# A gated mixture and a GRU on one core: first `up` products ahead of the routing, four banks, the sum's halves apart, step 0 without products

## The reference

```python
gate_logits = concat([full_agg, hp_agg, wp_agg]) @ gate_w + gate_b
gate_logits = gate_logits * (1.0 + scale) + shift      # from silu(cond) @ time_w + time_b
w_be = top-2 of softmax(gate_logits), normalised       # one weight per sequence and expert
for e in range(E):
    h = gelu(x @ ew1[e] + eb1[e])                      # 256 -> 1024
    out += w_be[:, e] * mask[e] * (h @ ew2[e] + eb2[e])
x = x + out + gelu(x @ sw1 + sb1) @ sw2 + sb2
def step(h, ...):                                      # 1024 steps, h0 = 0
    z = sigmoid(xz + h @ U_z + vz); r = sigmoid(xr + h @ U_r + vr)
    hh = tanh(xh + (r * h) @ U + vh)
    return (1 - z) * h + z * hh
x = x + scan(step, x)
```

## Time and profile before

| | us |
|---|---|
| median of 3 runs | 1881.32 |
| lowest, highest | 1879.59, 1881.68 |
| the profiled execution | 1878.24 |
| its span, first to last instruction | 1876.4 |

### The profile page before, as it was taken

How to read it: one execution, slowest core, us unless ns; L and a number is a source line. 1 busy time by engine, 2 the same in 40 slices (tenths; PEclk the granted TensorE clock), 3 DMA queues, 4 the chain that set the end, 5 groups by cost and what they waited for, 6 DMA issues and landing times.

```text
span 1876.4 us, 101766 instructions
## 1 busy us (share of the span) xinstructions
PE 1844.4 (98%) x39969; PEld 1703.9 (91%) x39970; DVE 1454.8 (78%) x11505; ACT 713.4 (38%) x3785; POOL 199.4 (11%) x515
## 2 busy tenths in 40 slices
PE   8999999999999999999999999999999999999998
PEld 8998999989899998999989999899999989999766
DVE  5787878778787787877878787787877878788776
ACT  4333433434333343433434344343433434334322
POOL 0110101101020110101101011110101101011000
PEclk9999999999999999999999999999999999999999
DMA  9000000000000000000000000000000000000000
GB/s 321 4 4 5 5 4 5 5 4 5 5 5 5 4 5 5 4 5 5 4 5 5 4 5 5 4 5 5 4 5 5 4 5 5 5 5 4 5 5 4
DMA packets 16926, 23.62 MB, mean 13 GB/s; under 512 B 3585, under 2 KB 15160, under 8 KB 16445
## 3 DMA queue, kind: packets, MB, share of 16 engines
q1 hardware_dynamic: 15280, 17.05, 2.6%
q10 hardware_dynamic: 1164, 0.07, 0.0%
HBM read 15.01 MB, written 2.10 MB: 9 GB/s over the span
## 4 chain that ended last, share of the span: by engine, by line
PE 94%; DVE 2%; ACT 2%; issue 1%; ACTq 0%; DVEq 0%
PE up_ps L740 20%; PE y_ps L758 20%; PE r_ps L863 13%; PE c_ps L863 13%; PE r_ps L842 6%; PE z_ps L863 6%; PE c_ps L842 5%; PE z_ps L872 4%; ACT rc_tanh_ps L408 2%; PE y_ps L690 2%; DVE h_cur L662 1%; PE c_ps L774 1%; PE z_ps L774 1%; DVE p_cur L633 1%; PE r_ps L774 1%
## 5 line engine op out<-in xcount | busy, mean ns | idle before, releaser
L740 PE MATMUL up_ps<-feat,up_w 128*128 128x128 f32 x2528 | 519.2, 302 | 0.2
L758 PE MATMUL y_ps<-hidden,down_w 128*128 128x128 f32 x2528 | 515.4, 301 | 0.0
L839 PEld LDWEIGHTS <-u_high 128*128 128x128 f16 x4096 | 398.2, 97 | 20.7
L408 ACT ACTIVATE rc_tanh_ps<-r_ps 128x4 f32<-128x4 f32 x1024 | 161.8, 158 | 574.5 <-PE r_ps L863 574.4
L740 PEld LDWEIGHTS up_ps<-feat,up_w 128*128 128x128 f32 x2528 | 362.3, 190 | 1.2 <-ACT hidden L397 0.9
L758 PEld LDWEIGHTS y_ps<-hidden,down_w 128*128 128x128 f32 x2528 | 360.4, 190 | 0.0
L863 PEld LDWEIGHTS r_ps<-h_cur,u_mid 128*128 128x128 f16 x4096 | 252.1, 96 | 113.6 <-issue 46.6
L863 PE MATMUL c_ps<-p_cur,u_mid 128*128 128x40 bf16 (+10 forms) x4096 | 337.4, 179 | 0.0
L863 PE MATMUL r_ps<-h_cur,u_mid 128*128 128x20 bf16 (+5 forms) x4096 | 336.4, 178 | 0.0
L662 DVE TENSOR_TENSOR_SCAN h_cur<-rc_tanh_ps,blend 128x8 f32<-128x8 f32 x1024 | 178.0, 174 | 165.5 <-ACT rc_tanh_ps L408 165.4
L288 POOL TENSOR_TENSOR hidden<-hidden,expert_w 128x128 f32<-128x128 f32 (+3 forms) x416 | 163.9, 394 | 1339.0 <-ACT hidden L397 1339.0
(11 more groups left out here) (154 smaller groups left out, 4059.0 us busy)
## 6 DMA issues: line engine op xcount, KB each, us to landing
up_w<-in_L_cond_ew SPq DMA_DIRECT2D x4, 1024.0 KB, 9.3
down_w<-in_L_cond_ew SPq DMA_DIRECT2D x4, 1024.0 KB, 10.4
x_rows<-in_x SPq DMA_DIRECT2D x8, 256.0 KB, 4.6
out<-out_rows SPq DMA_DIRECT2D x128, 16.0 KB, 1.8
up_w<-in_L_cond_sw SPq DMA_DIRECT2D x1, 1024.0 KB, 12.7
down_w<-in_L_cond_sw SPq DMA_DIRECT2D x1, 1024.0 KB, 13.4
cf<-in_L_cond_C_r SPq DMA_DIRECT2D x1, 256.0 KB, 9.6
cf<-in_L_cond_C_z SPq DMA_DIRECT2D x1, 256.0 KB, 9.4
```

Of the source, the lines that this page charges most:

```text
L408: act.activation((tanh_r, tanh_z, c_now)[g].rearrange("p (m b) -> p m b", b=B), before_tanh, ACT.Tanh, scale=0.5 / GAIN).then_inc(act_done, 1)
L740: last = mm(up_ps[n % 2][:, 0:COLS], up_w[:, e, k, j * P:(j + 1) * P], feat[:, k, c * COLS:(c + 1) * COLS], start=(k == 0), stop=(k == KC ...
L758: last = mm(y_ps[:, m * COLS:(m + 1) * COLS], down_w[:, e, j, m * P:(m + 1) * P], hidden[:, n % TILES_HELD, :], start=False, stop=(m == KC ...
L839: pe.ldweights(w[:, g, k, m * P:(m + 1) * P])
```

## The change

- Loads: x's first two (a quarter of x), then the first `up_w`, the rest of x, the second `up_w`; the `gate_in` loads go from ScalarE's queue to SP's, four ahead of `cf` and three behind `uf`; `down_w` and `up_w` in another order.
- Front on PE: eight fillers first, then x tiles 0 and 1, the small rows, `up` tiles 0 to 3, the other x tiles among tiles 4 to 6; the conditioning row and the logits behind tile 13, `cond_part` with five fillers behind tile 15, the expert weights behind tile 19. All of tiles 0 to 23 come ahead of the first `down`. Their banks are four: `up_ps` and, until seeded, `gate_ps` of Z and C. `hidden` holds 24 tiles.
- The two halves of the first chunk's sum go to two banks (`y_cols`); the last 8 tiles are summed for half 0 first, then for half 1, and each half has its own residual.
- Step 0: its R, Z and C products are left out, since the state is zero; `preact` is counted by the projections instead. `places` gives window (0, 0) no unit.
- VectorE and ScalarE do the same work in another order. The gelus of copies, the exp behind gelu 15 and the scaling of `wx` behind all gelus.

The diff, cut:

```diff
-TILES_HELD = 12
-FIRST_LAG = 10
+TILES_HELD = 24
+FRONT_BANKS_TO = 24
+WARM_FRONT = 8
-    places = lambda t, w: 1 + w - ((t, w) in TURNS)
+    places = lambda t, w: 0 if (t, w) == (0, 0) else 1 + w - ((t, w) in TURNS)
...
+        EXP_BEHIND = 15
+        FRONT_BANKS = [*up_ps, gate_ps[Z], gate_ps[C]]
+        def up_bank(n):
+            return FRONT_BANKS[n % 4] if n < FRONT_BANKS_TO else up_ps[n % 2]
+        def gelus_before_up(n):
+            return max([i + 1 for i in range(max(n - 4, 0), n) if up_bank(i) is up_bank(n)], default=0)
+        def y_cols(c, m):
+            return z_tanh_ps[:, 0:COLS] if c == 0 and m == 1 else y_ps[:, m * COLS:(m + 1) * COLS]
...
+            load_x(0)
             load_up(first[0])
+            for i in range(1, XT // 2):
+                load_x(i)
             load_up(first[1])
+            sp.dma_start(gate_w_sb[:, :, :, :], ...).then_inc(gate_in, 16)
+            sp.dma_start(time_w_sb[:, :, :], ...).then_inc(gate_in, 16)
+            sp.dma_start(bias_row[:, 0:2 * E], ...).then_inc(gate_in, 16)
+            sp.dma_start(bias_row[:, 2 * E:3 * E], ...).then_inc(gate_in, 16)
             load_mats(cf, c_in, cond_mats_in)
             load_mats(uf, u_in, u_in_sem)
+            sp.dma_start(mask_rows[:, :], branch_mask).then_inc(gate_in, 16)
+            sp.wait_ge(rows_cleared, 1)
+            sp.dma_start(bias2_rows[0:E, :], eb2).then_inc(gate_in, 16)
+            sp.dma_start(bias2_rows[E:BR, :], ...).then_inc(gate_in, 16)
...
+            COPIES_BEHIND = {1: (2, 3), 2: (4, 5), 3: (6, 7)}
             for i in range(len(TILES[0])):
                 gelu(0, i)
+                for tile in COPIES_BEHIND.get(i, ()):
+                    copy_x(tile)
+                if i == EXP_BEHIND:
...
             def residual(c, k):
-                if k == 0:
+                if k == 0 and c == 0:
+                    dve.wait_ge(first_sum_done, 1)
+                if k == 0 and c > 0 or k == 1 and c == 0:
                     dve.wait_ge(down_done, TILE0[c + 1])
...
-                    if n >= 2:
-                        pe.wait_ge(gelu_done, n - 1)
+                    if gelus_before_up(n):
+                        pe.wait_ge(gelu_done, gelus_before_up(n))
...
+            for i in range(WARM_FRONT):
+                idle_front(IDLE_FILL[1], start=(i == 0))
+            turn_x(0)
+            turn_x(1)
...
+            ups(0, 4)
+            turn_x(2)
+            turn_x(3)
+            ups(4, 5)
...
+            ups(8, 14)
+            time_row()
+            logit_row()
+            ups(14, 16)
+            cond_part(R)
+            cond_part(Z)
+            cond_part(C).then_inc(gbias_summed, 1)
+            ups(16, 20)
+            pe.wait_ge(spread_made, 1)
...
+            ups(20, 24)
...
+            late = first_tiles - HT
+            for i in range(late):
+                if HT <= i < 2 * HT:
+                    ups(late + i - HT, late + i - HT + 1)
+                for m in range(KC):
+                    down(0, i, m)
...
             for m in range(KC):
-                down(0, first_tiles - 1, m)
+                for i in range(late, first_tiles):
+                    last = down(0, i, m)
+                if m == 0:
+                    last.then_inc(first_sum_done, 1)
...
+                    if k == KC - 1:
+                        last.then_inc(preact, 1)
...
             for s in range(T):
                 c, t = divmod(s, CT)
                 parts = s * PARTS_STEP
+                if s == 0:
+                    side(c, t, 0)
+                    side(c, t, 1)
+                    continue
```

## The result

| | before | after |
|---|---|---|
| median of 10 runs, us | 1881.1 | 1885.76 |
| the profiled execution | 1878.24 | 1884.44 |
| its span | 1876.4 | 1882.6 |
| first scan of the state | 53.9 | 53.1 |
| step 0 of a chunk (1 to 14) | 1.84 | 1.78 |

The changed kernel is 0.3% slower: ratio 1.0029, 95% interval 1.0021 to 1.0037. Line 682 is the scan now, 769 `up`, 787 `down`, 805 `project`, 412 the gelu, 687 `half_h`, 692 `out_feat`, 653 `p_cur`, 923 most R, Z and C products.

A forecast was written before the change was run, and what follows sets the result against it. Each step was taken as bound by the chain scan, R products, tanh, C products, tanh, not by PE. Terms -2.3 + 5.7 + 3.6 - 1.0 = +6.0 us: 1884.2 for the profiled run, 1887.3 on the median; range 1881.5 to 1891.

The forecast's parts named there:

- bank wait: Window (3, 1): tile 3's `up` product waits for gelu 1 to free its bank; 0.38 us a chunk, 5.7 us.
- double scaling: Step 4's gelus 2 and 3 make GpSimd scale two tiles in a row; `p_cur` 0.24 us late, 3.6 us in 15 chunks.
- Rival C: Window (3, 1): the gelu ends before PE asks, so the wait costs nothing; faster, 1878.0 us; chance 0.10.
- rival B: GpSimd's second scaling costs nothing, as VectorE may slip between the two: +2.4, 1883.7 us; chance 0.20.
- Step 0 of the later chunks: Chunks 1 to 14: a filler replaces an `up` product in step 0, 1.84 to 1.78 us, 1.0 us saved.
- The front's end: First residual and projections no longer wait, 0.63 us saved; step 0 without products, 1.2 us saved.
- The front's start: First `up` near 8, PE waits at `time_row` for `gate_in` until 20.4, `down` ends at 48.4: 0.5 us saved.
- Rival D: Half-clock spells in the loop come oftener; five times would be +5 us, 1892; chance 0.08.

The follow-up runs named there:

- the table alone: The kernel before with only the new table of side units (window (0, 0) of each chunk empty): 1887.0 us, ratio 1.0040.

## Why the prediction was right, point by point

The direction, the place and the mechanism of the loss hold: a bank wait and a double scaling in each chunk. 1887.3 was forecast, 1885.76 came. That the sum lies so near is in part luck, since two of its terms were off in opposite directions.

- **The bank wait.** Forecast 0.38 us in 15 chunks, 5.7; measured 0.40, 6.0. It is shown three ways: by the weight load that names its releaser, by the table alone, and by moving gelu 1 alone. Rival C, that PE never asks before the gelu ends, is out.
- **The double scaling.** Forecast 0.24, 3.6 us; measured 0.11, 1.7 us. The mechanism was right: `out_feat` ends with the second scaling (at 1.28 behind C's tanh by the scan's place, forecast 1.32), in each of the 15 chunks. `p_cur` itself took 0.15, so only what stands ahead of it was slowed, as I took it. The mis-sized term is the step from there to `p_cur`, which I let start at `out_feat`'s end; it starts 0.07 ahead of it, and GpSimd does two scalings in 0.76, not 0.80. The rival B, nothing at all, is out, since step 5 goes back to 1.78 when the scalings are apart.
- **Step 0 of the later chunks.** Forecast and measured 0.07 us, 1.0 in all.
- **The front's end.** Residual and step 0: forecast 0.63 + 1.2, measured 49.52 - 48.89 = 0.63 gone and 1.46 - 0.32 = 1.14 (1.05 by the run that puts the products back). What was late next was not C's tanh but Z's chain: Z's tanh at 52.58, `blend` behind it, the scan 0.1 later than I put it.
- **The front's start** is the step that failed: end of `down` forecast at 48.4, measured 48.06 + 1.87 = 49.93. The sum from the row on was right (28.0, measured 27.8). The row came at 22.10, not at 20.4, for two reasons that met. `gate_in` lands later than the `uf` loads did before (at 21.6 to 22.4 in the traces that load it on SP's queue): I took 20.4 from the last `uf` load's 20.1, but that load is now issued at 16.39 and not at 12.29, behind four small ones on whose issue SP is from 8.0 to 12.1 us, and lands at 21.64. And PE's own path was not 19.5. I had the first `up` near 8, but its weights landed at 9.6: the later x loads moved at the same time (I had counted only the 1.6 MB issued ahead; in 9.7 us some 2.2 MB had moved, and no row shows the 2.5 us that I put ahead of the first byte). From there to the row I had 11.4 us; it took 12.4, since the small rows held PE idle to 8.07 and half clock followed, and 10.2 with fillers in that idle time. The sentence of the Trainium skill that only issue time is saved, usually small beside the transfer ("DMA: Bandwidth & Descriptors", "Issuing engines are not separate DMA queues"), is not what these runs show: the last of the small loads is issued at 18.09 on SP's queue, behind all the loads ahead of it, and at 6.94 on ScalarE's. With the clock kept up, PE waits 1.55 us for them in the first case and not at all in the second, not even where it reaches the row at 20.39 (the kernel with step 0's products put back).
- **The sum.** Front -0.8, bank 6.0, scaling 1.7, step 0 -1.0: 5.9, where the spans differ by 6.2 and the medians by 4.7. The sum came near 6.0 because the front's missing 1.5 us and the scaling's surplus of 1.9 cancel. The spans also differ by the half-clock spell of the earlier trace rows, about 1 us, which this trace of after does not have; it is made up by about 1 ns a step over the loop, which differs from execution to execution and which no run here explains, and by 0.2 behind the last scan.
- **Rival D, the clock in the loop,** is not in this trace: the granted clock is 1.00 from 14.8 to 1878.5 us. It does show in the spread: the four longest of the ten executions (1886.65 to 1891.18) have a mean granted clock of 0.992 to 0.994, the other six (1884.44 to 1885.79) of 0.996 to 0.998.

## What to carry to other kernels

When work is dealt out in order into slots beside a latency chain, taking one slot away moves everything behind it; work out, for every unit, how far it stands from what frees its buffer, and look for the one that now asks in the same step. Such a delay recurs with every round and outweighs a gain at the start that is had once. And a small load moved to a queue in order takes its place behind everything issued there: here the last of the `gate_in` loads, of 1 KB, landed at 22.05, 0.4 us behind the last of the `uf` loads ahead of it, and was issued at 17.65, where ScalarE had issued it at 6.08.

## What the runs showed of the hardware

A VectorE instruction with two SBUF inputs that is queued while GpSimd works does not get in between two GpSimd instructions that follow each other: `out_feat` took 0.43 to 0.44 us in the 15 steps with two whole scalings in a row, never over 0.40 in any other, 0.21 with one. `half_h`, which reads `h_cur` alone, took 0.39 beside a scaling and 0.16 without.

PE was idle from 5.5 to 8.1 us after a busy start. The granted clock fell to 0.50 at 8.0, still in that idle time, and stayed there for 6.8 us. The idle time in itself cost nothing, as the first weights landed only at 9.6; what came behind it did: 12.4 us from the first `up` to the row, against 10.2 where fillers stood in the idle time.

Early in an execution a granted clock of 1.00 is no proof of full speed. In the kernel with gelu 1 early, whose front is the same, a stretch reads 1.00 (the first number behind GpSimd's, as in the earlier trace rows) and yet eight `up` products take 2.05 us, as at 0.50 in the changed kernel, and not 1.13:

```profile
9.50:12.00 2.50, 2.08 (x9) 1.56 (x8) 1.57 (x4) 0.51 (x2) 0.00 (x0) 1.00 1.10 376
```
```profile
10.46 2.05 PE L771 MATMUL up_ps<-feat,up_w 128*128 128x128 f32 x8 [0.42 <-DMA up_w<-in_L_cond_ew]
```
